# Two graph layers on one core: natural layout of q and k, all score terms as paired half-height products, two head pairs per phase, a new step order

## The chip, the cores and the metric

The kernel runs on one core of one Trainium2 chip. The metric is device time in microseconds of one execution. Engines are named as the profile does: PE is TensorE, DVE is VectorE, ACT is ScalarE, POOL is GpSimd, SP issues the DMAs.

## The reference

64 samples of 256 nodes with 512 features, one 256x256 adjacency for all. Two layers, each with a residual and a layer norm:

```
mi, mj = x @ Wi.T, x @ Wj.T                      # W = [Wi | Wj]
h = layernorm(x + deg * (mi + b) + adj @ mj)
q, k, v = h @ Wq.T + bq, h @ Wk.T + bk, h @ Wv.T + bv   # 8 heads of 64
p = softmax(where(adj == 0, -inf, q @ k.T / 8))
out = layernorm(h + (p @ v) @ Wo.T + bo)
```

All in float32.

## The kernel before

Each float32 operand of a product is kept as two parts in the reduced format (hi and lo), and a product is three: hi*hi, lo*hi, hi*lo (`product`, L349 is the one line that issues them). P = 128 rows, R = 2 row tiles of a sample, C = 4 column tiles, G = 4 groups g of two heads (i = 0, 1), HALF = 64 rows is one head.

One step b works on two samples, and its previous one: the attention of sample b, the first layer and the projections q, k, v of sample n = b + 1, and the output product y and norm of sample b - 1. Every engine runs a list of helpers written out by hand (`step`), and they meet at semaphores only. `steps` runs step 0 without y, then 62 more in a loop or behind it, the last of them without loading ahead, and `last_step` finishes the attention of sample 63. The prologue loads and splits the weights and makes sample 0's h, q, k, v.

PE's order within a step decides when everything is needed: mj, mi (x times Wj, Wi), aggregate (adjacency times mj), transpose_h, q, k, v, y; and for each group of heads scores, transpose_p, attend. PSUM has eight banks: three for the projections in turn, two for scores (one a head), two for transposed probabilities (`pt`), one for `av`.

How a group of heads goes: scores on PE; `maxima` on DVE adds the mask, takes the row maximum, and makes exp_bias; `exponentials` on ACT (four activations of 128x256); `inverse_sums` on DVE; the even head is normalised on ACT, the odd on POOL; transpose_p on PE; `pt_high` on ACT and `pt_low` on DVE make hi and lo; attend on PE; then `o_low_part` (ACT), `o_sum` (DVE, into the single buffer oT), `o_high` (ACT), `split_o` (POOL). `o_sum` of group g waits until `split_o` of group g - 1 has read oT:

```
dve.wait_ge(o_part_done, G * b + g + 1)
if not (first and g == 0):
    dve.wait_ge(o_split, G * b + g)
```

For h: `agg_sum`, `norm_stats`, `norm_mean` on DVE, `root` on POOL, `norm_apply` on DVE, transpose_h on PE, `hT_high` on ACT, `hT_low` on DVE, and q on PE, which waits for both halves:

```
if half == 0:
    pe.wait_ge(read["hT"], 2 * n + 2)
```

POOL also splits the next x transposed: `xT_high` and `split_xT` of sample b + 2.

Layout of q and k before: for each head q_both holds hi on the head's own 64 rows and lo on the other 64; k_twice holds hi on both, the second copy made by DMA (`copy_k`, four a step). So one product of full height gives hi*hi + lo*hi (L475), and a product of half height adds q hi times k lo (L480). The order of the step of PE before stands in the diff.

## Time and profile before

| what | value |
|---|---|
| median of 3 runs | 3146.48 us (3145.89 to 3148.19) |
| span of the profiled execution, first to last instruction | 3145.9 us |
| busy: PE, DVE, ACT, POOL | 3097.3, 2451.1, 1960.7, 1154.5 us |
| weight loads of PE | 2715.3 us |
| mean granted clock of PE | 0.993 of full |

A whole time of the profiled execution is not given beside its span; the span stands 0.6 us under the median of the runs. Matmuls are pipelined, so busy PE says only that a product was always in flight. Instructions of a group that follow each other are merged in a timeline; its second column runs from the first start to the last end.

### The profile page before, as it was taken

Reading aid. Unit: us, or ns where it says so; the run is one execution under the profiler, and the core shown is the slowest. Engines: PE = TensorE matmul, PEld = TensorE weight load, DVE = VectorE, ACT = ScalarE, POOL = GpSimd, SP = SyncE. Lnnn points to the kernel's source line nnn. Section 1 sums busy time; section 2 is a strip of 40 time slices with the busy share of each in tenths; the row PEclk is TensorE's granted clock in tenths of the full one; section 3 lists DMA queues with packets and bytes.
Section 4 is the critical chain, followed back from the end, with each engine's and each line's share of the span. In section 5 each row is a group of like instructions: output and inputs, shape, how many; then the busy total and the mean of one; then the engine's idle time right before and its main releaser. Section 6 shows DMA issues by size and latency. Waiting matters only on the chain.

```text
span 3145.9 us, 59689 instructions
## 1 busy us (share of the span) xinstructions
PE 3097.3 (98%) x19456; PEld 2715.3 (86%) x19456; DVE 2451.1 (78%) x6156; ACT 1960.7 (62%) x4999; POOL 1154.5 (37%) x1097
## 2 busy tenths in 40 slices
PE   6999999999999999999999999999999999999997
PEld 5888888888888888888888888888888888888886
DVE  5778778778778787787787787877877878778776
ACT  3656666666566566666665666666656656666665
POOL 2333333433433333334333333333343333333432
PEclk8999999999999999999999999999999999999999
DMA  4011011111110110111111101111111111011110
GB/s 134 25 51 53 27 53 43 37 53 33 47 53 27 53 53 27 53 36 44 53 32 48 53 27 53 49 31 53 33 47 53 29 51 53 27 53 41 39 48 28
DMA packets 109868, 141.95 MB, mean 45 GB/s; under 512 B 7696, under 2 KB 73744, under 8 KB 109840
## 3 DMA queue, kind: packets, MB, share of 16 engines
q1 hardware_dynamic: 109840, 141.59, 15.2%
q8 instruction: 15, 0.25, 0.0%
q14 instruction: 13, 0.11, 0.0%
HBM read 74.46 MB, written 33.55 MB: 34 GB/s over the span
## 4 chain that ended last, share of the span: by engine, by line
PE 98%; DVE 1%; ACT 0%; issue 0%; DMA 0%; POOL 0%; POOLq 0%; DVEq 0%; SPq 0%
PE proj L349 73%; PE av L349 8%; PE pt L492 7%; PE score L475 4%; PE score L480 3%; PE proj L426 2%; DMA probs<-in_w0T 0%; DVE h L875 0%; DVE k_lo L786 0%; DVE probs L808 0%; DVE pT_lo L823 0%; DVE oT L832 0%; DVE wj_lo L927 0%; DVE wo_lo L927 0%; POOL var_eps_h L284 0%
## 5 line engine op out<-in xcount | busy, mean ns | idle before, releaser
L639 ACT ACTIVATE probs<-probs,exp_bias 128x256 f32<-128x256 f32 x1024 | 509.2, 499 | 247.2 <-DVE exp_bias L814 247.2
L292 POOL TENSOR_TENSOR oT_lo<-oT,oT_hi 128x256 fp32r<-128x256 f32 x256 | 189.8, 742 | 949.3 <-ACT oT_hi L669 949.3
L808 DVE CUSTOM_DVE_ANT_0 probs<-score,mask_add 128x256 f32<-128x256 f32 x1024 | 371.6, 420 | 86.2 <-PE score L480 42.2
L259 POOL TENSOR_TENSOR probs<-probs,row_inv 128x512 f32<-128x512 f32 x256 | 267.0, 1043 | 459.3 <-DVE row_inv L819 459.3
L648 ACT ACTIVATE probs<-probs,row_inv 128x256 f32<-128x256 f32 x512 | 234.2, 509 | 236.9 <-DVE row_inv L819 236.9
L655 ACT CAST pT_hi<-pt 128x512 fp32r<-128x512 f32 x512 | 280.4, 587 | 160.3 <-PE av L349 97.1
L823 DVE TENSOR_TENSOR pT_lo<-pt,pT_hi 128x512 fp32r<-128x512 f32 x512 | 333.5, 681 | 6.1 <-ACT pT_hi L655 0.2
L844 DVE SCALAR_TENSOR_TENSOR h<-proj,deg,xb 128x512 f32<-128x512 f32 x128 | 96.0, 751 | 254.2 <-PE proj L349 254.2
L786 DVE SCALAR_TENSOR_TENSOR q_both<-proj,bq_cols,q_both 64x256 fp32r<-64x256 f32 x512 | 247.6, 484 | 56.3 <-ACT q_both L617 48.7
L349 PE MATMUL proj<-hT_hi,wq_hi 128*128 128x256 f32 x1024 | 289.2, 282 | 1.5 <-DVE hT_lo L764 1.5
L349 PE MATMUL proj<-hT_hi,wq_lo 128*128 128x256 f32 x1024 | 289.0, 282 | 0.0
L349 PE MATMUL proj<-hT_lo,wq_hi 128*128 128x256 f32 x1024 | 288.8, 282 | 0.0
L349 PE MATMUL proj<-hT_hi,wk_lo 128*128 128x256 f32 x1024 | 287.9, 281 | 0.0
L349 PE MATMUL proj<-hT_hi,wk_hi 128*128 128x256 f32 x1024 | 287.5, 281 | 0.0
L349 PE MATMUL proj<-hT_lo,wk_hi 128*128 128x256 f32 x1024 | 287.5, 281 | 0.0
L492 PE MATMUL pt<-ident,probs 128*128 128x128 f32 x2048 | 281.8, 276 | 2.5 <-ACT probs L648 2.5
L349 PE MATMUL av<-pT_hi,v_both 128*128 128x256 f32 x1024 | 271.5, 297 | 4.2 <-DVE pT_lo L823 4.2
L832 DVE SCALAR_TENSOR_TENSOR oT<-av,bv_cols,o_part 64x256 f32<-64x256 f32 x512 | 243.0, 475 | 34.1 <-POOL oT_lo L292 24.9
L786 DVE SCALAR_TENSOR_TENSOR k_lo<-proj,bk_cols,k_twice 64x256 fp32r<-64x256 f32 x512 | 247.5, 483 | 18.3 <-ACT k_twice L629 2.3
L349 PE MATMUL av<-pT_lo,v_both 128*128 128x256 f32 x1024 | 255.5, 283 | 0.0
L492 PEld LDWEIGHTS pt<-ident,probs 128*128 128x128 f32 x2048 | 233.4, 142 | 20.6 <-ACT probs L648 3.0
L617 ACT ACTIVATE q_both<-proj,bq_cols 64x256 fp32r<-64x256 f32 x512 | 241.1, 471 | 15.5 <-PE proj L349 7.5
(98 smaller groups left out, 8826.6 us busy)
## 6 DMA issues: line engine op xcount, KB each, us to landing
xT_raw<-in_xT SPq DMA_DIRECT2D x64, 512.0 KB, 4.5
xb<-in_x SPq DMA_DIRECT2D x64, 512.0 KB, 5.2
k_twice<-k_twice SPq DMA_DIRECT2D x256, 128.0 KB, 2.4
out<-hb SPq DMA_DIRECT2D x64, 512.0 KB, 3.3
probs<-in_w0T SPq DMA_DIRECT2D x1, 1024.0 KB, 6.8
hb<-in_w0T SPq DMA_DIRECT2D x1, 1024.0 KB, 9.0
probs<-in_wqT SPq DMA_DIRECT2D x1, 1024.0 KB, 5.5
hb<-in_wkT SPq DMA_DIRECT2D x1, 1024.0 KB, 5.8
```

The source lines that it names most:

```text
L259: pool.tensor_tensor(probs[:, g % 2, 1, :, :], probs[:, g % 2, 1, :, :], row_inv[:, g % 2, R:2 * R].unsqueeze(2).to_broadcast([P, R, N]), ...
L292: pool.tensor_tensor(oT_lo[:, g, :], oT[:, :], oT_hi[:, g, :].bitcast(F32), ALU.subtract).then_inc(o_split, 1)
L349: return pe.matmul(dst, lhsT, rhs, start=start, stop=stop)
L492: last = pe.transpose(dst[:, kt, r * P:(r + 1) * P], probs[:, g % 2, i, r, kt * P:(kt + 1) * P], ident[:, :])
L617: last = nc.scalar.activation(q_both[home, 2 * t + i, :], src[home, :], ACT.Identity, bias=bq_cols[home, t:t + 1])
L639: last = nc.scalar.activation(e, e, ACT.Exp, bias=exp_bias[:, g % 2, s:s + 1], scale=SCALE, accum_out=row_sum[:, g % 2, s:s + 1])
L648: last = nc.scalar.activation(e, e, ACT.Copy, scale=row_inv[:, g % 2, r:r + 1])
L655: nc.scalar.copy(pT_hi[:, i, :, :], pt[i][:, :].rearrange("p (k q) -> p k q", k=R)).then_inc(pt_hi_done, 1)
L786: last = V.scalar_tensor_tensor(out=dst(t, i), in0=src[home, :], scalar=bias[home, t:t + 1], in1=high[home, 2 * t + i, :].bitcast(F32), op ...
L808: last = V.tensor_tensor_reduce(out=probs[:, g % 2, i, r, :], in0=score[i][:, r * N:(r + 1) * N], in1=mask_add[:, r, :], scale=1.0, scalar ...
L823: V.tensor_tensor(pT_lo[:, i, :, :], pt[i][:, :].rearrange("p (k q) -> p k q", k=R), pT_hi[:, i, :, :].bitcast(F32), ALU.subtract).then_in ...
L832: last = V.scalar_tensor_tensor(out=oT[i * HALF:(i + 1) * HALF, :], in0=av[0:HALF, i * N:(i + 1) * N], scalar=bv_cols[:, 2 * g + i:2 * g + ...
```

## The change

q and k lie in natural layout: q_hi, q_lo, k_hi, k_lo, each 128 rows by column tile, two heads one above the other. The bias-and-split helpers work on 128 rows at once, two instructions a half where there were four, and the DMA copies of k are gone. All three terms of a score are half-height products; the two heads of a group are issued in pairs, rows 0 to 63 and 64 to 127, into two banks. `scores` now covers two groups at once (24 products) and is called twice a step. Scores and transposed probabilities share four banks `attn`, two for each group parity: the scores of groups 2 and 3 wait until `pt_low` of group 1 has read its bank. The order of the step changes on PE, ACT, DVE and POOL; the last step's likewise (left out here, with the bank names in maxima, pt_high and pt_low).

```diff
@@ -94,8 +94,9 @@
-        q_both = sb("q_both", [P, HEADS, N], F32R)
-        k_twice = sb("k_twice", [P, HEADS, N], F32R)
+        q_hi = sb("q_hi", [P, C, N], F32R)
+        q_lo = sb("q_lo", [P, C, N], F32R)
+        k_hi = sb("k_hi", [P, C, N], F32R)
         k_lo = sb("k_lo", [P, C, N], F32R)
...
@@ -126,8 +127,8 @@
-        score = [bank(f"score{i}") for i in range(2)]
-        pt = [bank(f"pt{i}") for i in range(2)]
+        attn = [bank(f"attn{i}") for i in range(4)]
         av = bank("av")
...
@@ -190,22 +190,12 @@
...
-            def copy_k(n, half):
...
-                    sp.dma_start(k_twice[(1 - i) * HALF:(2 - i) * HALF, heads, :].bitcast(F32),
-                                 k_twice[i * HALF:(i + 1) * HALF, heads, :].bitcast(F32)).then_inc(k_copied[half], 16)
...
@@ -315,15 +303,15 @@
                 n = b + 1
                 add_bias(n)
                 normalise_odd(b, 0)
+                normalise_odd(b, 1)
                 root("h", n)
-                normalise_odd(b, 1)
-                normalise_odd(b, 2)
                 if ahead: xT_high(b + 2)
                 if ahead: split_xT(b + 2)
                 split_o(b, 0)
+                split_o(b, 1)
+                normalise_odd(b, 2)
                 normalise_odd(b, 3)
                 if y_: root("out", b - 1)
-                split_o(b, 1)
                 split_o(b, 2)
                 residual(n, 1 - parity, stored=y_)
...
@@ -461,32 +449,28 @@
...
-            def scores(b, g, first=False):
-                pe.wait_ge(read["q"], 2 * b + g // 2 + 1)
-                pe.wait_ge(read["k"], 2 * b + g // 2 + 1)
-                pe.wait_ge(k_copied[g // 2], 32 * (b + 1))
-                if not (first and g == 0):
-                    pe.wait_ge(max_done, 2 * (G * b + g))
-                blocks = [(i, r) for i in range(2) for r in range(R)]
-                for i, r in blocks:
-                    head = 2 * g + i
-                    pe.matmul(score[i][:, r * N:(r + 1) * N], q_both[:, head, r * P:(r + 1) * P],
-                              k_twice[:, head, :], start=(r == 0), stop=False, skip_group_check=True)
-                for i, r in [(i, r) for r in range(R) for i in range(2)]:
-                    head, home = 2 * g + i, slice(i * HALF, (i + 1) * HALF)
-                    last = pe.matmul(score[i][:, r * N:(r + 1) * N], q_both[home, head, r * P:(r + 1) * P],
-                                     k_lo[home, g, :], start=False, stop=True, skip_group_check=True)
-                    if r == R - 1:
-                        last.then_inc(score_done, 1)
-            def transpose_p(b, g, i, first=False):
+            def scores(b, pair, first=False):
+                pe.wait_ge(read["q"], 2 * b + pair + 1)
+                pe.wait_ge(read["k"], 2 * b + pair + 1)
+                if not (first and pair == 0):
+                    pe.wait_ge(pt_read, 2 * (G * b + 2 * pair))
+                for g in (2 * pair, 2 * pair + 1):
+                    terms = [(q_hi, k_hi), (q_lo, k_hi), (q_hi, k_lo)]
+                    for r in range(R):
+                        for j, (q_, k_) in enumerate(terms):
+                            for i in range(2):
+                                home = slice(i * HALF, (i + 1) * HALF)
+                                last = pe.matmul(attn[2 * (g % 2) + i][:, r * N:(r + 1) * N],
+                                                 q_[home, g, r * P:(r + 1) * P], k_[home, g, :],
+                                                 start=(r == 0 and j == 0), stop=(j == len(terms) - 1),
+                                                 skip_group_check=True)
+                                if r == R - 1 and j == len(terms) - 1:
+                                    last.then_inc(score_done, 1)
+            def transpose_p(b, g, i):
                 pe.wait_ge((norm_even_done, norm_odd_done)[i], G * b + g + 1)
-                if not (first and g == 0):
-                    pe.wait_ge(pt_read, 2 * (G * b + g) + i - 1)
-                dst = pt[i][:, :].rearrange("p (k q) -> p k q", k=R)
+                dst = attn[2 * (g % 2) + i][:, :].rearrange("p (k q) -> p k q", k=R)
...
@@ -513,34 +497,32 @@
                 scores(b, 0, not y_)
                 mj(n, 1)
                 mi(n, 0)
-                scores(b, 1)
                 mi(n, 1)
+                transpose_p(b, 0, 0)
+                transpose_p(b, 0, 1)
                 aggregate(n, 0)
                 aggregate(n, 1)
-                transpose_p(b, 0, 0, not y_)
-                transpose_p(b, 0, 1, not y_)
-                scores(b, 2)
+                attend(b, 0, not y_)
+                transpose_p(b, 1, 0)
+                transpose_p(b, 1, 1)
                 if y_: y(b - 1, 0)
+                attend(b, 1)
+                scores(b, 1)
                 if y_: y(b - 1, 1)
                 transpose_h(n, 0)
                 transpose_h(n, 1)
-                scores(b, 3)
-                transpose_p(b, 1, 0)
-                transpose_p(b, 1, 1)
-                attend(b, 0, not y_)
                 q(n, 0)
                 q(n, 1)
                 transpose_p(b, 2, 0)
                 transpose_p(b, 2, 1)
-                attend(b, 1)
                 k(n, 0)
+                attend(b, 2)
+                transpose_p(b, 3, 0)
+                transpose_p(b, 3, 1)
                 k(n, 1)
-                transpose_p(b, 3, 0)
-                attend(b, 2)
-                transpose_p(b, 3, 1)
+                attend(b, 3)
                 v(n, 0)
                 v(n, 1)
-                attend(b, 3)
...
@@ -606,29 +586,20 @@
...
-            def q_high(n, half):
+            def biased_high(kind, n, half, bias, dst):
                 heads_used(n, half)
-                act.wait_ge(done["q"], 2 * n + half + 1)
+                act.wait_ge(done[kind], 2 * n + half + 1)
                 for c in range(2):
                     t = 2 * half + c
-                    src = proj[BANK["q"][half]][:, c * N:(c + 1) * N]
-                    for i in range(2):
-                        home = slice(i * HALF, (i + 1) * HALF)
-                        last = nc.scalar.activation(q_both[home, 2 * t + i, :], src[home, :], ACT.Identity,
-                                                    bias=bq_cols[home, t:t + 1])
-                last.then_inc(hi["q"], 1)
+                    last = nc.scalar.activation(dst[:, t, :], proj[BANK[kind][half]][:, c * N:(c + 1) * N],
+                                                ACT.Identity, bias=bias[:, t:t + 1])
+                last.then_inc(hi[kind], 1)
+            def q_high(n, half):
+                biased_high("q", n, half, bq_cols, q_hi)
             def k_high(n, half):
...
+                biased_high("k", n, half, bk_cols, k_hi)
...
@@ -673,37 +645,37 @@
                 mj_high(n, 0)
                 exponentials(b, 0)
                 mj_high(n, 1)
+                exponentials(b, 1)
                 normalise_even(b, 0)
-                exponentials(b, 1)
+                normalise_even(b, 1)
                 pt_high(b, 0, 0, not y_)
-                normalise_even(b, 1)
                 pt_high(b, 0, 1, not y_)
+                o_low_part(b, 0, not y_)
+                pt_high(b, 1, 0)
+                pt_high(b, 1, 1)
+                o_high(b, 0, not y_)
+                o_low_part(b, 1)
                 exponentials(b, 2)
+                o_high(b, 1)
                 hT_high(n, 0)
                 hT_high(n, 1)
+                exponentials(b, 3)
                 normalise_even(b, 2)
-                pt_high(b, 1, 0)
-                pt_high(b, 1, 1)
-                o_low_part(b, 0, not y_)
-                exponentials(b, 3)
                 q_high(n, 0)
+                normalise_even(b, 3)
                 q_high(n, 1)
-                o_high(b, 0, not y_)
-                o_low_part(b, 1)
                 pt_high(b, 2, 0)
                 pt_high(b, 2, 1)
-                normalise_even(b, 3)
                 k_high(n, 0)
-                k_high(n, 1)
-                o_high(b, 1)
+                o_low_part(b, 2)
                 pt_high(b, 3, 0)
                 pt_high(b, 3, 1)
-                o_low_part(b, 2)
+                o_high(b, 2)
+                k_high(n, 1)
+                o_low_part(b, 3)
+                o_high(b, 3)
                 v_high(n, 0)
                 v_high(n, 1)
-                o_high(b, 2)
-                o_low_part(b, 3)
-                o_high(b, 3)
...
@@ -780,33 +752,29 @@
                 dve.wait_ge(hi[kind], 2 * n + half + 1)
                 for c in range(2):
                     t = 2 * half + c
-                    src = proj[BANK[kind][half]][:, c * N:(c + 1) * N]
-                    for i in range(2):
-                        home = slice(i * HALF, (i + 1) * HALF)
-                        last = V.scalar_tensor_tensor(
-                            out=dst(t, i), in0=src[home, :], scalar=bias[home, t:t + 1],
-                            in1=high[home, 2 * t + i, :].bitcast(F32), op0=ALU.add, op1=ALU.subtract)
+                    last = V.scalar_tensor_tensor(
+                        out=dst[:, t, :], in0=proj[BANK[kind][half]][:, c * N:(c + 1) * N], scalar=bias[:, t:t + 1],
+                        in1=high[:, t, :].bitcast(F32), op0=ALU.add, op1=ALU.subtract)
                 last.then_inc(read[kind], 1)
             def q_low(n, half):
-                biased_low("q", n, half, bq_cols, q_both,
-                           lambda t, i: q_both[(1 - i) * HALF:(2 - i) * HALF, 2 * t + i, :])
+                biased_low("q", n, half, bq_cols, q_hi, q_lo)
             def k_low_half(n, half):
-                biased_low("k", n, half, bk_cols, k_twice,
-                           lambda t, i: k_lo[i * HALF:(i + 1) * HALF, t, :])
+                biased_low("k", n, half, bk_cols, k_hi, k_lo)
...
@@ -877,50 +846,50 @@
             def step(b, parity, y_=True, ahead=True):
                 n, other = b + 1, 1 - parity
+                mj_low(n, 0)
                 maxima(b, 0, not y_)
-                mj_low(n, 0)
-                mi_sum(n, 0)
+                maxima(b, 1, not y_)
                 mj_low(n, 1)
                 inverse_sums(b, 0)
-                maxima(b, 1, not y_)
+                mi_sum(n, 0)
+                inverse_sums(b, 1)
                 mi_sum(n, 1)
+                pt_low(b, 0, 0)
+                pt_low(b, 0, 1)
                 agg_sum(n, 0)
                 agg_sum(n, 1)
                 norm_stats("h", n, 0, read["agg"], h_row)
                 norm_stats("h", n, 1, read["agg"], h_row)
-                inverse_sums(b, 1)
                 norm_mean("h", n)
-                maxima(b, 2)
+                o_sum(b, 0, not y_)
+                pt_low(b, 1, 0)
+                pt_low(b, 1, 1)
                 norm_apply("h", n, h_row)
                 if y_: y_sum(b - 1, 0, other)
-                pt_low(b, 0, 0)
-                pt_low(b, 0, 1)
+                o_sum(b, 1)
+                maxima(b, 2)
+                if y_: norm_stats("out", b - 1, 0, read["y"], hb_row[other])
+                maxima(b, 3)
                 if y_: y_sum(b - 1, 1, other)
-                inverse_sums(b, 2)
                 hT_low(n, 0)
                 hT_low(n, 1)
-                maxima(b, 3)
-                if y_: norm_stats("out", b - 1, 0, read["y"], hb_row[other])
-                pt_low(b, 1, 0)
-                pt_low(b, 1, 1)
-                o_sum(b, 0, not y_)
+                inverse_sums(b, 2)
+                if y_: norm_stats("out", b - 1, 1, read["y"], hb_row[other])
+                if y_: norm_mean("out", b - 1)
                 inverse_sums(b, 3)
-                if y_: norm_stats("out", b - 1, 1, read["y"], hb_row[other])
                 q_low(n, 0)
+                if y_: norm_apply("out", b - 1, hb_row[other])
                 q_low(n, 1)
-                o_sum(b, 1)
                 pt_low(b, 2, 0)
                 pt_low(b, 2, 1)
-                if y_: norm_mean("out", b - 1)
                 k_low_half(n, 0)
+                o_sum(b, 2)
+                pt_low(b, 3, 0)
+                pt_low(b, 3, 1)
                 k_low_half(n, 1)
-                pt_low(b, 3, 0)
-                o_sum(b, 2)
-                pt_low(b, 3, 1)
-                if y_: norm_apply("out", b - 1, hb_row[other])
+                o_sum(b, 3)
                 v_low(n, 0)
                 v_low(n, 1)
-                o_sum(b, 3)
```

## Rows read from the trace of the kernel before

**Rows 1.** The page, part 4: share of the chain that ended last.

```profile
PE 98%; DVE 1%; ACT 0%; issue 0%; DMA 0%; POOL 0%; POOLq 0%; DVEq 0%; SPq 0%
```

**Rows 2.** The chain in order of time: start us, us, what.

```profile
1480.28 5.79 PE proj L349 x24
1528.44 5.79 PE proj L349 x24
```

**Rows 3.** Timeline of PE, a score group: start us, us, what, idle before.

```profile
1514.02 0.64 PE L475 MATMUL score<-k_twice,q_both 128*128 128x256 f32 x4
1514.59 0.50 PE L480 MATMUL score<-k_lo,q_both 64*128 64x256 f32 x4
1515.02 0.50 PE L349 MATMUL proj<-wj_hi,xT_hi 128*128 128x512 f32 x1
1515.36 0.39 PE L349 MATMUL proj<-wj_hi,xT_lo 128*128 128x512 f32 x1
```

**Rows 4.** Line 480 in 1510 to 1524: ns min/median/max.

```profile
L480 PE MATMUL score<-k_lo,q_both x8: 277/330/383, 1514.6 to 1521.5; 64*128 64x256 f32 x8
```

**Rows 5.** Timeline of ACT.

```profile
1534.70 1.07 ACT L589 CAST hT_hi<-proj 128x512 fp32r<-128x512 f32 x2 [1.57 <-PE proj L426]
...
1540.55 0.51 ACT L639 ACTIVATE probs<-probs,exp_bias 128x256 f32<-128x256 f32 x1 [0.80 <-DVE exp_bias L814]
...
1542.45 0.19 ACT L639 ACTIVATION_READ_ACCUMULATOR probs<-probs,exp_bias 128x1 f32 x1
1542.66 3.87 ACT L617 ACTIVATE q_both<-proj,bq_cols 64x256 fp32r<-64x256 f32 x8
```

**Rows 6.** Timeline of DVE.

```profile
1522.43 0.40 DVE L808 CUSTOM_DVE_ANT_0 probs<-score,mask_add 128x256 f32<-128x256 f32 x1
...
1523.90 0.17 DVE L814 TENSOR_SCALAR exp_bias<-row_max 128x4 f32<-128x4 f32 x1
...
1526.69 0.69 DVE L850 TENSOR_TENSOR h<-proj,h 128x512 f32<-128x512 f32 x1 [0.25 <-PE proj L349]
1527.30 1.27 DVE L864 BATCH_NORM_STATS2 stats_h<-h 128x6 f32<-128x512 f32 x2
...
1528.68 0.25 DVE L870 BATCH_NORM_AGGREGATE mean_var_h<-stats_h 128x2 f32<-128x6 f32 x2
...
1532.45 1.27 DVE L823 TENSOR_TENSOR pT_lo<-pt,pT_hi 128x512 fp32r<-128x512 f32 x2
...
1535.32 1.29 DVE L764 TENSOR_TENSOR hT_lo<-proj,hT_hi 128x512 fp32r<-128x512 f32 x2 [0.28 <-ACT hT_hi L589]
...
1542.22 0.96 DVE L832 SCALAR_TENSOR_TENSOR oT<-av,bv_cols,o_part 64x256 f32<-64x256 f32 x2
...
1544.62 3.99 DVE L786 SCALAR_TENSOR_TENSOR q_both<-proj,bq_cols,q_both 64x256 fp32r<-64x256 f32 x8 [0.65 <-ACT q_both L617]
```

**Rows 7.** Timeline of PE, transpose_h.

```profile
1534.07 1.04 PE L426 MATMUL proj<-ident,h 128*128 128x128 f32 x8
```

**Rows 8.** Timeline of POOL.

```profile
1529.28 0.70 POOL L287 TENSOR_TENSOR rstd_h<-var_eps_h,power_cols 128x2 f32<-128x2 f32 x1
...
1536.12 1.90 POOL L252 TENSOR_TENSOR xT_hi<-xT_raw,zero 128x1024 fp32r<-128x1024 f32 x1
1538.10 2.39 POOL L265 TENSOR_TENSOR xT_lo<-xT_raw,xT_hi 128x1024 fp32r<-128x1024 f32 x1
1547.04 0.73 POOL L292 TENSOR_TENSOR oT_lo<-oT,oT_hi 128x256 fp32r<-128x256 f32 x1 [6.55 <-ACT oT_hi L669]
```

**Rows 9.** Timeline of DVE in the prologue.

```profile
34.30 4.58 DVE L875 TENSOR_SCALAR h<-h,mean_var_h,rstd_h 128x512 f32<-128x512 f32 x2 [0.87 <-POOL rstd_h L287]
```

**Rows 10.** Timeline of PE in the first step.

```profile
86.50 1.97 PE L426 MATMUL proj<-ident,h 128*128 128x128 f32 x8 [3.55 <-DVE h L875]
```

**Rows 11.** PE by stretches: window, length, busy us (instructions), granted clock, DMA share, GB/s.

```profile
84.00:86.00 2.00, 0.00 (x0) 0.92 0.00 0
...
92.00:94.00 2.00, 2.00 (x17) 0.87 0.00 0
```

More of the change, by code:

```diff
@@ L191, in store @@
                 sp.dma_start(out_rows[b, :, :, :], hb[:, parity, :, :]).then_inc(out_stored, 16)
-            def copy_k(n, half):
-                sp.wait_ge(hi["k"], 2 * n + half + 1)
-                for i in range(2):
-                    heads = slice(4 * half + i, 4 * half + i + 3, 2)
-                    sp.dma_start(k_twice[(1 - i) * HALF:(2 - i) * HALF, heads, :].bitcast(F32),
-                                 k_twice[i * HALF:(i + 1) * HALF, heads, :].bitcast(F32)).then_inc(k_copied[half], 16)
             def step(b, parity, y_=True, ahead=True):
@@ L333, in last_step @@
                 normalise_odd(b, 1)
+                split_o(b, 0)
+                split_o(b, 1)
                 normalise_odd(b, 2)
-                split_o(b, 0)
                 normalise_odd(b, 3)
+                split_o(b, 2)
                 root("out", b - 1)
-                split_o(b, 1)
-                split_o(b, 2)
                 split_o(b, 3)
@@ L562, in last_step @@
                 scores(b, 0)
-                scores(b, 1)
+                y(b - 1, 0, tail=True)
                 transpose_p(b, 0, 0)
                 transpose_p(b, 0, 1)
-                scores(b, 2)
-                y(b - 1, 0, tail=True)
-                scores(b, 3)
+                attend(b, 0)
                 transpose_p(b, 1, 0)
                 transpose_p(b, 1, 1)
-                attend(b, 0)
                 y(b - 1, 1, tail=True)
+                scores(b, 1)
+                attend(b, 1)
                 transpose_p(b, 2, 0)
-                attend(b, 1)
                 transpose_p(b, 2, 1)
@@ L655, in pt_high @@
                 nc.scalar.copy(pT_hi[:, i, :, :],
-                               pt[i][:, :].rearrange("p (k q) -> p k q", k=R)).then_inc(pt_hi_done, 1)
+                               attn[2 * (g % 2) + i][:, :].rearrange("p (k q) -> p k q",
+                                                                     k=R)).then_inc(pt_hi_done, 1)
             def o_low_part(b, g, first=False):
@@ L734, in last_step @@
                 normalise_even(b, 1)
-                exponentials(b, 2)
-                normalise_even(b, 2)
+                o_low_part(b, 0)
                 pt_high(b, 1, 0)
                 pt_high(b, 1, 1)
-                o_low_part(b, 0)
+                o_high(b, 0)
+                exponentials(b, 2)
+                o_low_part(b, 1)
+                normalise_even(b, 2)
                 exponentials(b, 3)
-                o_high(b, 0)
-                o_low_part(b, 1)
+                o_high(b, 1)
                 pt_high(b, 2, 0)
                 pt_high(b, 2, 1)
-                o_high(b, 1)
                 normalise_even(b, 3)
@@ L808, in maxima @@
                         last = V.tensor_tensor_reduce(
-                            out=probs[:, g % 2, i, r, :], in0=score[i][:, r * N:(r + 1) * N],
+                            out=probs[:, g % 2, i, r, :], in0=attn[2 * (g % 2) + i][:, r * N:(r + 1) * N],
                             in1=mask_add[:, r, :], scale=1.0, scalar=MASKED, op0=ALU.add, op1=ALU.max,
@@ L822, in pt_low @@
                 dve.wait_ge(pt_hi_done, 2 * (G * b + g) + i + 1)
-                V.tensor_tensor(pT_lo[:, i, :, :], pt[i][:, :].rearrange("p (k q) -> p k q", k=R),
+                V.tensor_tensor(pT_lo[:, i, :, :],
+                                attn[2 * (g % 2) + i][:, :].rearrange("p (k q) -> p k q", k=R),
                                 pT_hi[:, i, :, :].bitcast(F32), ALU.subtract).then_inc(pt_read, 1)
@@ L970, in last_step @@
                 maxima(b, 1)
+                y_sum(b - 1, 0, 0)
                 inverse_sums(b, 1)
-                maxima(b, 2)
                 pt_low(b, 0, 0)
                 pt_low(b, 0, 1)
-                y_sum(b - 1, 0, 0)
+                norm_stats("out", b - 1, 0, read["y"], hb_row[0])
+                o_sum(b, 0)
+                pt_low(b, 1, 0)
+                pt_low(b, 1, 1)
+                maxima(b, 2)
                 inverse_sums(b, 2)
                 maxima(b, 3)
-                pt_low(b, 1, 0)
-                pt_low(b, 1, 1)
-                o_sum(b, 0)
-                norm_stats("out", b - 1, 0, read["y"], hb_row[0])
-                y_sum(b - 1, 1, 0)
+                o_sum(b, 1)
                 inverse_sums(b, 3)
-                norm_stats("out", b - 1, 1, read["y"], hb_row[0])
-                norm_mean("out", b - 1)
-                o_sum(b, 1)
                 pt_low(b, 2, 0)
                 pt_low(b, 2, 1)
-                norm_apply("out", b - 1, hb_row[0])
+                y_sum(b - 1, 1, 0)
+                norm_stats("out", b - 1, 1, read["y"], hb_row[0])
                 o_sum(b, 2)
+                norm_mean("out", b - 1)
                 pt_low(b, 3, 0)
                 pt_low(b, 3, 1)
+                norm_apply("out", b - 1, hb_row[0])
                 o_sum(b, 3)
```

16 lines of the change are left out of this document (removed).

## The prediction

> **What bounds the kernel now.** I read the chain that ended last first: TensorE (PE) holds 98% of it [rows 1]. Two equal pieces of the loop, a step apart, stand 48.16 us from each other [rows 2]. So a step costs what its TensorE instructions cost, end to end, and everything else is cover. The 24 products in that piece take 5.79 us with the last one lasting 0.40, so a product of 512 columns comes every 0.234 us [rows 2]. Two questions decide: does TensorE get less to do, and does the new order still keep every other engine ahead of it?
>
> **TensorE's work.** One group of scores before: four full-height products start at 14.02, four half-height ones at 14.59, the next block at 15.02, whose first product takes 0.34 us to the next start instead of 0.234 [rows 3]. That is 1.00 + 0.11 = 1.11 us a group, 4.44 a step. The full ones come every (0.64 - 0.28)/3 = 0.12 us. The half-height ones are the question. Their record is 0.50 us for four, the longest 383 ns, the shortest 277 [rows 3, 4]: four in a row at 0.12 would need 0.28 + 3 x 0.12 = 0.64, so two run side by side, and the second pair ends 0.50 - 0.383 = 0.117 us behind the first. The extra 0.106 of the long ones is a weight load laid bare when the height changes. What is left of the 1.11, after 4 x 0.12 and 2 x 0.117, is 0.40: two changes of height at 0.20 each.
> After: 24 half-height products a phase are 12 pairs, 12 x 0.117 + 0.40 = 1.80 us, twice a step 3.60. TensorE gets 0.84 us less a step: 47.32 us. All of it comes from two phases instead of four, that is 4 changes of height fewer (0.80); the products themselves come out even (6 slots a group before and after). Bounds: a pair at 0.12 gives -0.77; a pair at 0.222, if weight loads could not hide behind the pair before, gives +1.7.
> The rule that speaks against this: the Trainium skill, "TensorE: Matmul & The Clock Gate", part 3 (packing small matmuls), says a weight load overlaps running matmuls only where the row group differs. By that rule every second pair would lay its load bare, 0.117 + 0.106 = 0.22 us a pair, and the sum would be 5.3 + 0.8 = 6.1 us a step instead of 3.60. The row of this kernel has the second pair 0.117 us behind the first in the same row groups, so I go by the row; it is one sample of two pairs, and so a rival.
>
> **ScalarE, VectorE, queues.** q_high and k_high fall from 16 activations a step to 8, the lows likewise: eight of q take 3.87 us on ScalarE and eight 3.99 on VectorE [rows 5, 6], and the same for k, so each engine loses about 3.9 us a step. They lie beside TensorE and are worth nothing there by themselves. In the prologue they stand on the chain: half of one q_high, of one q_low and of k_low is about 4 us, once. Four k copies a step leave the SP queue; what was queued behind them (store, next xT and x loads) only goes earlier, and I give it nothing.
>
> **The new order.** Here I laid the steps out one behind the other. Mark zero is the end of the first transpose_p of group 0. TensorE's own work from there to the end of transpose_h is: second transpose 4 x 0.11 = 0.44 (eight take 1.04, the last 0.28: 0.11 each [rows 7]), aggregate 8 x 0.234 = 1.87, attend 0 0.95, transposes of group 1 0.87, y0 2.81, attend 1 0.95, scores 1.80, y1 2.81, transpose_h 0.87. Sum 13.37 us. And q(n,0) now stands directly behind transpose_h, where before scores(3), two transposes and attend(0) lay between (1.11 + 0.87 + 0.95, 2.9 us of products). q waits for hT_lo.
> The work that leads to hT_lo, from the same mark:
> - pt_high 0.03 + 0.59 (a cast of 128x512; two take 1.07 [rows 5]): 0.62.
> - VectorE without a pause: pt_low twice, 1.2 (two in 1.27), to 1.85; agg_sum twice, 0.61 to the next start each, to 3.06; norm_stats twice, done at 4.33; norm_mean 0.11 + 0.25, done at 4.69 [rows 6].
> - root("h") on POOL: norm_mean's end (1528.93) to rstd's end (1529.98) is 1.05: 5.74 [rows 6, 8].
> - Now POOL has xT_high and split_xT next, 1536.12 to 1540.49, 4.37 us: 10.11. Only then split_o(0), 0.73: 10.84 [rows 8]. Before, these two sat in a quiet place behind normalise_odd(2), and split_o(0) had a wide margin to its reader.
> - o_sum(1) waits for split_o(0), because oT is one buffer, and in VectorE's order maxima(2) stands behind o_sum(1). o_sum 0.06 + 0.9: 11.80 [rows 6]. Meanwhile VectorE sits in norm_apply("h"): in the prologue, under the very same xT_high and split_xT, its two instructions took 4.58 us [rows 9] instead of about 1; this blocking ends when split_xT does, so it costs nothing beyond the gate of split_o(0).
> - maxima(2): 1522.43 to 1523.90 + 0.17 = 1.64 [rows 6]: bias at 13.44. Then on VectorE norm_stats 0.6, maxima(3) 1.6, y_sum(1) 0.6: free at 16.2. On ScalarE exponentials(2) 1540.55 to 1542.64, 2.09: 15.56; o_high(1) 0.3, an estimate from the activations of the same width less their fixed part: 15.85; hT_high(0) 0.59, hT_high(1) 0.48 more: 16.95.
> - hT_low(0) from 16.4, hT_low(1) from 17.0, done at 17.7 [rows 6]; q's first product is late by hand-over 0.07, bare weight load 0.106 and its own length 0.277, less the 0.12 it would take anyway: 0.33. Together 18.03 us.
> TensorE stands 18.03 - 13.37 = 4.66 us a step. A few tenths of it fall before attend(1), whose pt_low(1,1) stands behind the same VectorE run; nearly all before q. The other waits just hold. Transposes of group 0: counted from the end of mj(0), mj_high and mj_low take 1.25, maxima(0) 1.64, exponentials(0) 2.1, mj_high(1) 0.5, exponentials(1) 2.0, normalise_even about 1.0 (half an exponentials), together 8.5; TensorE arrives after 1.80 + 3 x 2.81 = 10.2. The same count leaves attend 0, 2 and 3 a few tenths each, so the rest of the step adds nothing in my layout; plus or minus 0.5 for hand-overs.
> The Trainium skill, "SBUF — State Buffer", section on the two separate sides, has VectorE's two-port instructions and GpSimd lock each other out for a whole instruction; [rows 9] agrees, and by rule and row the sum is the same here.
>
> **The clock.** In the first step of before TensorE stood 3.55 us ahead of transpose_h, until 86.50 [rows 10]. The granted clock averages 0.92 in 84 to 86 and 0.87 in 92 to 94 [rows 11], so it was at half (1.2 of 2.4 GHz) from about 85.7 to 92.5; about 6.0 us of products ran in it and lost 3.0. A stall of over 4 us in every step will do the same again and again, and the products behind it (q, k, then the next step up to the transposes) are on the loop. Bounds per step 0 and 3.0; I take 1.7, since with a longer stall more of the low stretch lies inside the idleness, and only dense products follow.
>
> **Sum.** 47.32 + 4.66 + 1.7 = 53.7 us a step against 48.16: +5.5. 62 full steps: +343 us; prologue -4; the last two steps I leave as they are (plus or minus 10). The profiled span of 3145.9 stands 0.6 us under the median of 3146.48, so 3146.5 + 343 - 4 = 3486 us. A change under 0.2% (6 us) could not be told from none.
>
> **Rivals.**
> 1. The gate through split_o, with the clock falling: 3486 us, its own range 3420 to 3550. Chance 0.52.
> 2. The same gate, but the clock holds or nearly: +3.8 x 62, about 3380. For it: stalls shorter than a microsecond or so leave the clock alone; against it: 3.55 us did not. 0.17.
> 3. Only the direct conversion shows: hT_high and hT_low behind transpose_h take 0.59 + 0.48 + 0.69 + 0.33 less the half transpose already over (0.44), 1.7 us, if POOL gets to split_o earlier than laid out or maxima slip ahead. Then 47.3 + 1.7 + 0.3 = 49.3, 3220 without and 3320 with the clock. 0.13.
> 4. Weight loads of pairs lie bare (0.22 us a pair): the first phase lies on the loop, +1.3 a step; the second is absorbed by the stall. 3565. 0.12.
> 5. The other side: all waits are covered and the 0.84 us remain, 3146 - 52 - 4 = 3090. This needs hT_lo done 0.3 us before transpose_h ends; the conversion alone forbids it by 1.7 us, so it decides only if TensorE is late elsewhere. 0.03. Near no change, the two cancelling (stall under 0.9 us): 0.03.
> Faster 0.03, same 0.02, slower 0.95. The range runs from the upper part of rival 3 to rival 4: 3320 to 3575.
>
> **What would show it.** Per step: an idle stretch of TensorE of 4 to 5 us before the first q product, released by hT_lo of VectorE; VectorE's norm_apply("h") in pairs far over 1 us; oT on VectorE waiting for oT_lo of POOL; TensorE's clock under 1 in the middle slices; two score groups a step with pairs ending 0.12 us apart. Wrong if split_o(0) is done before VectorE comes to o_sum(1), if the stall lies before attend or the transposes instead, if pairs end 0.22 us apart, or if the granted clock stays at 1.0.

## The result and the profile after

The changed kernel takes 3767.7 us against 3146.7 us: a ratio of 1.1975 (95% interval 1.1961 to 1.1989), 19.7% slower. The forecast was slower, 3486 us, with 3575 as its upper end; the time lies 282 us above it.

The chain that ended last, first line of the page's part 4, the one that gave TensorE 98% before [rows 1]:

```profile
PE 73%; DVE 14%; ACT 6%; issue 4%; POOL 2%; DMA 0%; DVEq 0%; SPq 0%; POOLq 0%; ACTq 0%
```

So 27% of that chain is no longer TensorE's. Two pieces of the chain in order of time (start us, us, what), 41 steps apart:

```profile
236.15 8.59 PE proj L337 x36
...
2614.87 8.59 PE proj L337 x36
```

(2614.87 - 236.15) / 41 = 58.02 us a step, against 48.16 [rows 2]: 9.86 more, and 62 such steps are 611 of the 621 us. The loop explains the change; prologue and last steps are small. Timeline of PE in one step (idle before, and its releaser, in brackets):

```profile
1527.97 0.39 PE L337 MATMUL proj<-wo_lo,oT_hi 128*128 128x512 f32 x1
1528.47 0.38 PE L337 MATMUL av<-pT_hi,v_both 128*128 128x256 f32 x1
1528.69 0.28 PE L337 MATMUL av<-pT_lo,v_both 128*128 128x256 f32 x1
...
1529.61 0.39 PE L464 MATMUL attn<-k_hi,q_hi 64*128 64x256 f32 x2
1529.84 0.28 PE L464 MATMUL attn<-k_hi,q_lo 64*128 64x256 f32 x2
...
1531.02 0.28 PE L464 MATMUL attn<-k_lo,q_hi 64*128 64x256 f32 x2
1531.23 0.50 PE L337 MATMUL proj<-wo_hi,oT_hi 128*128 128x512 f32 x1
...
1533.90 0.39 PE L337 MATMUL proj<-wo_lo,oT_hi 128*128 128x512 f32 x1
1534.13 1.03 PE L414 MATMUL proj<-ident,h 128*128 128x128 f32 x8
1542.70 0.58 PE L337 MATMUL proj<-hT_hi,wq_hi 128*128 128x256 f32 x1 [7.53 <-DVE hT_lo L736]
1543.08 0.42 PE L337 MATMUL proj<-hT_hi,wq_lo 128*128 128x256 f32 x1
...
1547.99 0.34 PE L337 MATMUL proj<-hT_hi,wq_hi 128*128 128x256 f32 x1
```

Three things stand here. The scores of two groups run from 1529.61 to 1531.23, the first product behind them takes 0.11 us longer to the next start than the usual 0.234, and a change of height begins ahead of 1529.61 (0.09 us by the same count as in [rows 3]). The pair starts lie 0.12 us apart from the second pair on: the products cost what was forecast, 1.8 us a phase. Then transpose_h ends its stream, and TensorE stands 7.53 us until hT_lo is there. And q's first product takes 0.58 us, where 0.38 is what it takes behind a wait at the full clock (in e4 below): it runs at half the clock.

What happens during those 7.53 us is read on ScalarE, which had been idle before o_high(0) too:

```profile
1521.46 1.07 ACT L626 CAST pT_hi<-attn 128x512 fp32r<-128x512 f32 x2 [1.30 <-PE attn L476]
...
1534.33 0.41 ACT L641 CAST oT_hi<-oT 128x256 fp32r<-128x256 f32 x1 [7.92 <-PE proj L337]
1534.76 0.58 ACT L634 COPY o_part<-av 64x512 f32<-64x512 f32 x1
1538.35 0.51 ACT L610 ACTIVATE probs<-probs,exp_bias 128x256 f32<-128x256 f32 x1 [3.00 <-DVE exp_bias L782]
...
1540.33 0.39 ACT L641 CAST oT_hi<-oT 128x256 fp32r<-128x256 f32 x1
1540.74 1.07 ACT L569 CAST hT_hi<-proj 128x512 fp32r<-128x512 f32 x2
```

The bracket of the second row is the finding: o_high(0) (oT_hi) was released by PE proj, that is by y(b-1,1), whose last product ends at 1534.29 (1533.90 + 0.39), not by oT on VectorE. On POOL (same step) xT_lo was long over when split_o(0) came:

```profile
1529.20 2.45 POOL L253 TENSOR_TENSOR xT_lo<-xT_raw,xT_hi 128x1024 fp32r<-128x1024 f32 x1
1534.82 0.72 POOL L280 TENSOR_TENSOR oT_lo<-oT,oT_hi 128x256 fp32r<-128x256 f32 x1 [3.16 <-ACT oT_hi L641]
```

And on VectorE, from o_sum(0) on:

```profile
1526.12 0.97 DVE L801 SCALAR_TENSOR_TENSOR oT<-av,bv_cols,o_part 64x256 f32<-64x256 f32 x2
...
1528.33 3.61 DVE L844 TENSOR_SCALAR h<-h,mean_var_h,rstd_h 128x512 f32<-128x512 f32 x2
1531.86 0.68 DVE L825 TENSOR_TENSOR hb<-proj,hb 128x512 f32<-128x512 f32 x1
1535.64 0.97 DVE L801 SCALAR_TENSOR_TENSOR oT<-av,bv_cols,o_part 64x256 f32<-64x256 f32 x2 [3.11 <-POOL oT_lo L280]
1536.64 0.42 DVE L776 CUSTOM_DVE_ANT_0 probs<-attn,mask_add 128x256 f32<-128x256 f32 x1
...
1538.14 0.17 DVE L782 TENSOR_SCALAR exp_bias<-row_max 128x4 f32<-128x4 f32 x1
...
1540.47 0.69 DVE L825 TENSOR_TENSOR hb<-proj,hb 128x512 f32<-128x512 f32 x1
1541.36 1.29 DVE L736 TENSOR_TENSOR hT_lo<-proj,hT_hi 128x512 fp32r<-128x512 f32 x2 [0.20 <-ACT hT_hi L569]
```

o_sum(0) had oT ready at 1527.09, 7.2 us before o_high(0) took it. norm_apply took 3.61 us beside POOL's xT pair, as in [rows 9], y_sum(0) followed, and then o_sum(1) waited 3.11 us for split_o(0). Everything behind it in VectorE's order came late: maxima(2), maxima(3), y_sum(1), hT_low. PE by stretches of 2 us (window, length, busy, granted clock, DMA share, GB/s):

```profile
1536.00:1538.00 2.00, 0.00 (x0) 0.97 0.00 0
...
1542.00:1544.00 2.00, 1.30 (x6) 0.50 0.00 0
...
1548.00:1550.00 2.00, 2.00 (x18) 0.97 0.00 0
```

The clock is at half from just before 1538 to just past 1548 (0.97 in 1548 to 1550 is 0.12 us at half); half of q's products run in it.

The step adds up. From the end of transpose_h (1534.13 + 1.03) to the end of q's first product (1542.70 + 0.58) are 8.12 us, 8.0 more than the 0.12 it would take anyway. Of these, 0.2 are the clock (0.58 us instead of 0.38) and 7.8 are standing. attend(1) adds 0.37 of standing: its first product starts 0.50 us behind the last one of y(b-1,0) instead of 0.234, and takes 0.22 to the next start instead of 0.12. Together 8.2 us of standing. The 23 starts from 1543.08 to 1547.99 lie 0.213 us apart instead of 0.118, 2.2 us in all; with the 0.2 of the first product the clock costs 2.4. The products take 47.4, by e7 below: 47.4 + 8.2 + 2.4 = 58.0.

### The profile page after: what moved, and what is told of

Its sections match the earlier page's. It is cut to its first block, busy times and chain, and to the rows that moved or that the text cites. A ratio compares the mean times of both kernels' runs of the same rounds, so it can differ in the third digit from the quotient of the medians.

```text
span 3765.8 us, 59564 instructions
## 1 busy us (share of the span) xinstructions
PE 3232.9 (86%) x20480; PEld 2836.7 (75%) x20480; DVE 2209.1 (59%) x5644; ACT 1682.8 (45%) x4487; POOL 1159.8 (31%) x1097
## 4 chain that ended last, share of the span: by engine, by line
PE 73%; DVE 14%; ACT 6%; issue 4%; POOL 2%; DMA 0%; DVEq 0%; SPq 0%; POOLq 0%; ACTq 0%
PE proj L337 58%; PE attn L464 5%; PE av L337 5%; PE attn L476 4%; ACT probs L610 3%; DVE pT_lo L791 3%; DVE probs L776 2%; DVE hT_lo L736 2%; DVE h L819 2%; DVE stats_h L833 2%; DVE oT L801 2%; POOL oT_lo L280 1%; ACT oT_hi L641 1%; ACT hT_hi L569 1%; ACT pT_hi L626 1%
## 5 line engine op out<-in xcount | busy, mean ns | idle before, releaser
L337 PEld LDWEIGHTS proj<-hT_hi,wq_hi 128*128 128x128 f32 x1024 | 270.6, 264 | 492.3 <-DVE hT_lo L736 490.4
L776 DVE CUSTOM_DVE_ANT_0 probs<-attn,mask_add 128x256 f32<-128x256 f32 x1024 | 371.5, 419 | 14.1 <-PE attn L464 3.4
L641 ACT CAST oT_hi<-oT 128x256 fp32r<-128x256 f32 x256 | 102.8, 402 | 577.1 <-PE proj L337 495.4
L755 DVE SCALAR_TENSOR_TENSOR q_lo<-proj,bq_cols,q_hi 128x256 fp32r<-128x256 f32 x256 | 112.1, 479 | 399.1 <-ACT q_hi L594 399.1
L791 DVE TENSOR_TENSOR pT_lo<-attn,pT_hi 128x512 fp32r<-128x512 f32 x512 | 329.5, 685 | 26.3 <-ACT pT_hi L626 22.3
L626 ACT CAST pT_hi<-attn 128x512 fp32r<-128x512 f32 x512 | 275.1, 591 | 88.9 <-PE attn L476 85.6
L476 PE MATMUL attn<-ident,probs 128*128 128x128 f32 x2048 | 268.0, 274 | 8.7 <-ACT probs L619 5.2
L337 PEld LDWEIGHTS proj<-hT_hi,wq_lo 128*128 128x128 f32 x1024 | 268.9, 263 | 0.0
L337 PEld LDWEIGHTS proj<-hT_lo,wq_hi 128*128 128x128 f32 x1024 | 264.8, 259 | 0.0
L594 ACT ACTIVATE q_hi<-proj,bq_cols 128x256 fp32r<-128x256 f32 x256 | 107.3, 470 | 318.0 <-PE proj L337 318.0
```

The costliest lines, as they stand in the source:

```text
L337: return pe.matmul(dst, lhsT, rhs, start=start, stop=stop)
L476: last = pe.transpose(dst[:, kt, r * P:(r + 1) * P], probs[:, g % 2, i, r, kt * P:(kt + 1) * P], ident[:, :])
L626: nc.scalar.copy(pT_hi[:, i, :, :], attn[2 * (g % 2) + i][:, :].rearrange("p (k q) -> p k q", k=R)).then_inc(pt_hi_done, 1)
L641: nc.scalar.copy(oT_hi[:, g, :], oT[:, :]).then_inc(o_hi_done, 1)
L755: last = V.scalar_tensor_tensor(out=dst[:, t, :], in0=proj[BANK[kind][half]][:, c * N:(c + 1) * N], scalar=bias[:, t:t + 1], in1=high[:, t ...
L776: last = V.tensor_tensor_reduce(out=probs[:, g % 2, i, r, :], in0=attn[2 * (g % 2) + i][:, r * N:(r + 1) * N], in1=mask_add[:, r, :], scal ...
```

## The experiments

Two theories. A: the gate in front of o_sum(1) is o_high(b,0), which waits for the end of y(b-1,1), since y(b-1) still reads oT_hi and oT_lo:

```python
if g == 0 and not first:
    act.wait_ge(done["y"], R * b)
```

B, the prediction's own: POOL's xT_high and split_xT, put ahead of split_o(0), are the gate by themselves.

**e1_two_oT.** Two slots in turn for groups 0 and 1; a wait for y remains ahead of group 2, which has one slot:

```diff
-        oT_hi = sb("oT_hi", [P, G, N], F32R)
+        oT_hi = sb("oT_hi", [P, G + 2, N], F32R)
...
+        def slot(g, par):
+            return g if g >= 2 or par == 0 else G + g
...
-                if g == 0 and not first:
+                if g == 2 and not (type(b) is int and b == 0):
                     act.wait_ge(done["y"], R * b)
```

> The changed kernel with two slots in turn for groups 0 and 1 of oT_hi and oT_lo, so that o_high(b,0) no longer waits until y(b-1,1) has read them. Theory A (the gate in front of o_sum(1) is o_high(0), which waits for the end of y(b-1,1)): o_sum(1) comes free when split_xT ends, about 3.1 us a step earlier; TensorE's idle time before q falls from 7.5 to 4.4 us; 3767 - 61 x 3.1 = about 3578 us, plus or minus 60 for the clock. Theory B (the prediction's: POOL's xT_high and split_xT ahead of split_o(0) are the gate by themselves): nothing changes, 3767 us.

Measured 3556.6 us, ratio 1.1301 (1.1282 to 1.1320). POOL and PE in one of its steps:

```profile
1502.89 2.46 POOL L256 TENSOR_TENSOR xT_lo<-xT_raw,xT_hi 128x1024 fp32r<-128x1024 f32 x1
1505.31 0.92 POOL L283 TENSOR_TENSOR oT_lo<-oT,oT_hi 128x256 fp32r<-128x256 f32 x1
```

```profile
1513.39 0.58 PE L340 MATMUL proj<-hT_hi,wq_hi 128*128 128x256 f32 x1 [4.46 <-DVE hT_lo L739]
```

Now split_o(0) follows split_xT without a gap: the prediction's gate exists, but in the changed kernel it opened first (xT_lo ends at 1531.65) and o_high(0) held the way for another 3.2 us. Without the later gate the idle time before q is 4.46 us. A holds, B by itself does not.

**e2_pool_order.** split_o ahead of the xT pair, nothing else:

```diff
                 root("h", n)
+                split_o(b, 0)
+                split_o(b, 1)
                 if ahead: xT_high(b + 2)
                 if ahead: split_xT(b + 2)
-                split_o(b, 0)
-                split_o(b, 1)
                 normalise_odd(b, 2)
```

> The changed kernel with split_o(0) and split_o(1) moved ahead of xT_high and split_xT on POOL, nothing else. Theory A: the end of y(b-1,1) still releases o_high(0), so the time stays within 0.5% of 3767 us although norm_apply of h is no longer held up (its pair falls from 3.6 to about 1 us). Theory B: the gate opens 4.3 us earlier, about 3500 us.

Measured 3765.6 us, 1.1964 (1.1944 to 1.1984): unchanged. norm_apply of h fell from 3.61 to 0.99 us, and o_sum(1) waited 5.72 us for split_o(0) instead of 3.11. What norm_apply had lost beside POOL's xT pair fell into a time of waiting anyway. B, as the one cause, falls.

**e3_both.** Both edits.

> Both edits together: two slots for oT of groups 0 and 1, and split_o ahead of the xT pair. Theory A: the two gates lie one behind the other, so only now both are open; VectorE and ScalarE still run maxima(2), maxima(3), exponentials(2), hT_high and hT_low behind the scores; idle before q about 2.4 us, 3400 us plus or minus 60 for the clock. Theory B: the same as the pool order alone.

Measured 3342.0 us, 1.0620 (1.0603 to 1.0638), at the lower end of what was forecast. From 200 to 3000 us the granted clock, read in stretches of 1 us, falls 33 times, each time for 3.4 us. Steps with such a fall take 51.8 us, the others 50.3. TensorE's waits there, over 54 steps (who waited for whom, us in total, times, longest):

```profile
PE proj L340 <- DVE hT_lo L739: 120.3, 54, 2.2
```

2.2 us a step are left: the conversion of h itself and the maxima, exponentials and y_sum that stand in line ahead of it. e2's edit is worth nothing alone and 215 us behind e1's.

**e4_fill.** To price the clock alone: 20 products a step that nobody reads, between transpose_h and q.

```diff
+            def fill(b):
+                pe.wait_ge(av_read, G * b + 2)
+                for i in range(20):
+                    mm(av[:, :], w_hi["wk"][:, 0, 0:P], w_hi["wk"][:, 1, :], True, True)
...
                 transpose_h(n, 1)
+                fill(b)
                 q(n, 0)
```

> The changed kernel with 20 further products of 512 columns a step on TensorE between transpose_h and q, of weights into the bank av, whose result nobody reads; they start when o_sum(1) has read av (4.7 us of products in the idle stretch of 7.5 us). Clock theory (the halved clock over the first 5.5 us of q costs 2.7 us a step): the clock stays at full, q starts at the same time and runs faster, 3767 - 61 x 2.7 = about 3602 us, though there are 1280 products more. Rival (the low clock lies in the shade of some other wait): no gain, 3767 us or more.

Measured 3617.1 us, 1.1493 (1.1474 to 1.1512): 1260 products more make the kernel 150 us faster than the changed one. PE in one step:

```profile
1530.55 1.03 PE L414 MATMUL proj<-ident,h 128*128 128x128 f32 x8
1533.13 4.85 PE L337 MATMUL av<-wk_hi 128*128 128x512 f32 x20 [1.55 <-DVE oT L807]
1539.17 0.38 PE L337 MATMUL proj<-hT_hi,wq_hi 128*128 128x256 f32 x1 [1.19 <-DVE hT_lo L742]
```

transpose_h to q is 8.62 us, as good as the 8.57 of the changed kernel (1534.13 to 1542.70): the fill moved nothing. But q's first product takes 0.38 us, not 0.58. PE from 200 to 3400 us, this kernel and then the changed one (clock behind the busy time):

```profile
200.00:3400.00 3200.00, 3039.45 (x19583) 1.00 0.09 29
```

```profile
200.00:3400.00 3200.00, 2771.99 (x17612) 0.91 0.08 27
```

So of the step's 9.86 us, 2.4 (150 us over 62 steps) are the clock; the rest is 8.2 of standing still less 0.7 of cheaper products.

**e5_y_early.** Only TensorE's order: y(b-1,1) directly behind y(b-1,0).

```diff
                 if y_: y(b - 1, 0)
+                if y_: y(b - 1, 1)
                 attend(b, 1)
                 scores(b, 1)
-                if y_: y(b - 1, 1)
```

> The changed kernel with y(b-1,1) issued right behind y(b-1,0) on TensorE, ahead of attend(1) and scores(1), nothing else: no buffer and no other engine's order is touched. Theory A (o_high(0) is held by the end of y(b-1,1)): that end comes 2.8 us earlier, o_sum(1) as well, but the scores of groups 2 and 3 come 2.8 us later; q starts about 2 to 2.8 us earlier, 3767 - 61 x 2.5 = about 3615 us, less again if the low stretch of the clock shortens (down to 3560). Theory B (POOL's xT pair is the gate): 3767 us, since POOL's order is the same.

Measured 3556.6 us, 1.1299 (1.1281 to 1.1316), a little under the lower end that was forecast (3560). Moving the product that nobody seemed to wait for takes 211 us off, with POOL as it was. A holds again.

**e6_layout_only.** The kernel before, its order and banks, with the natural layout and the three paired terms, one group a phase.

```diff
-                blocks = [(i, r) for i in range(2) for r in range(R)]
...
+                terms = [(q_hi, k_hi), (q_lo, k_hi), (q_hi, k_lo)]
+                for r in range(R):
+                    for j, (q_, k_) in enumerate(terms):
+                        for i in range(2):
```

> The kernel before with the new layout alone: q_hi, q_lo, k_hi, k_lo in natural layout, three half-height products a term in pairs, no copies of k, but one group a phase, two score banks and the whole step order of before. Theory A (pairs end 0.117 us apart, a change of height costs 0.20 twice a phase): a group costs 6 x 0.117 + 0.40 = 1.10 us as before, so only the prologue gains, 3142 us, plus or minus 5. Rival (pairs lay their weight loads bare, 0.22 each): +2.5 us a step, 3300 us.

Measured 3143.2 us, ratio 0.9989 (0.9980 to 0.9998), within 0.2%. One group of scores on PE:

```profile
1507.85 0.39 PE L463 MATMUL score<-k_hi,q_hi 64*128 64x256 f32 x2
1508.07 0.28 PE L463 MATMUL score<-k_hi,q_lo 64*128 64x256 f32 x2
...
1508.54 0.28 PE L463 MATMUL score<-k_lo,q_hi 64*128 64x256 f32 x2
1508.76 0.50 PE L337 MATMUL proj<-wj_hi,xT_hi 128*128 128x512 f32 x1
1509.09 0.39 PE L337 MATMUL proj<-wj_hi,xT_lo 128*128 128x512 f32 x1
```

1507.85 to 1508.76 is 0.91, and the next product takes 0.34 to the following start instead of 0.234: 1.02 us a group. By starts this is under the 1.10 expected, since part of the first change of height lies ahead of 1507.85; a whole step takes 48.15 us, as before. The layout costs and gives nothing in the loop, as worked out. The first score products of step 0 start at 63.73 us, against 68.55 before, so the 4 us that the whole gains come from the prologue. The rival with bare weight loads is out.

**e7_reordered.** Can the change be kept without its waits? e3 with y(b-1,1) between transpose_h and q (q's banks swapped, so that only its second half waits until y is read), the conversion of h ahead of what does not hurry, and POOL's xT pair later. The edit is shown against e3's kernel; lines of moved helpers are left out where they stood.

```diff
-                "q": (1, 2), "k": (0, 1), "v": (2, 1)}
+                "q": (2, 1), "k": (0, 1), "v": (2, 1)}
...
                 if y_: root("out", b - 1)
+                if y_: pool.wait_ge(normed["out"], R * b)
+                if ahead: xT_high(b + 2)
+                if ahead: split_xT(b + 2)
...
                     pe.wait_ge(read["hT"], 2 * n + 2)
+                else:
                     if type(n) is not int or n >= 2:
...
-                    pe.wait_ge(read["q"], 2 * n + 1)
+                    pe.wait_ge(read["q"], 2 * n + 2)
...
                 scores(b, 1)
-                if y_: y(b - 1, 1, 1 - parity)
                 transpose_h(n, 0)
                 transpose_h(n, 1)
+                if y_: y(b - 1, 1, 1 - parity)
...
+                hT_high(n, 0)
+                hT_high(n, 1)
                 exponentials(b, 2)
...
                 maxima(b, 2)
+                hT_low(n, 0)
+                hT_low(n, 1)
```

> The changed kernel with two slots for oT of groups 0 and 1, y(b-1,1) between transpose_h and q on TensorE (q's banks swapped so that only its second half waits for y), hT_high ahead of exponentials(2), hT_low ahead of maxima(3), and the xT pair on POOL behind root of out and norm_apply of out. Theory A (all that the change lost is the waiting in front of q and the clock that falls with it; the products themselves are 0.84 us a step cheaper): TensorE never waits in a steady step, the clock stays at full, 47.3 us a step, 3146 - 62 x 0.84 - 4 = about 3090 us. Rival (shared banks or two groups a phase cost something of their own): above 3146 us.

Measured 3127.8 us, ratio 0.9932 (0.9918 to 0.9945): faster than before by 0.7%, 640 us under the changed kernel, but 38 us over the 3090 expected. A step takes 47.75 us (mean of six), and TensorE does wait once in it (weight loads):

```profile
1517.96 0.19 PEld L341 LDWEIGHTS av<-pT_hi,v_both 128*128 128x128 f32 x1 [0.51 <-DVE pT_lo L796]
```

That is attend(1), about 0.33 us end to end; without it the products are 47.4 us, 0.74 under before. The loop gains 0.41 x 62 = 25 us; 20 are left in the whole, so some 5 are given back outside it, where 4 from the prologue had been expected on top. A part lies at the end: from 3050 us on TensorE is granted 0.80 of its clock on average, against 0.92 in the kernel before. One of the five runs took 3121.5 us, at a mean granted clock of 0.994 instead of 0.991. I did not take these stretches apart further.

**e8_attend_early.** e7 with o_sum(0) and pt_low(1) ahead of norm_stats(1) and norm_mean on VectorE, and y_sum(0) ahead of norm_apply; the edit is shown against e7's kernel.

```diff
-                norm_stats("h", n, 1, read["agg"], h_row)
-                norm_mean("h", n)
                 o_sum(b, 0, not y_)
                 pt_low(b, 1, 0)
                 pt_low(b, 1, 1)
-                norm_apply("h", n, h_row)
+                norm_stats("h", n, 1, read["agg"], h_row)
+                norm_mean("h", n)
                 if y_: y_sum(b - 1, 0, other)
+                norm_apply("h", n, h_row)
```

> The reordered kernel with o_sum(0) and pt_low(1) moved ahead of the second norm_stats of h and norm_mean on VectorE, and y_sum(0) ahead of norm_apply. Theory A (the one wait left in a steady step is attend(1) for pt_low(1,1), 0.33 us end to end, the same that the prediction laid out): it goes, 47.4 us a step, 3128 - 62 x 0.33 = about 3107 us. Rival (norm_apply now comes too late for transpose_h): the wait moves there and the time stays at 3128 us or rises.

Measured 3142.2 us, 0.9987 (0.9978 to 0.9996): the rival. The one wait has become two:

```profile
1526.55 0.86 PEld L418 LDWEIGHTS proj<-ident,h 128*128 128x128 f32 x8 [0.40 <-DVE h L849]
...
1530.33 0.19 PEld L341 LDWEIGHTS proj<-hT_hi,wq_hi 128*128 128x128 f32 x1 [0.32 <-DVE hT_lo L741]
```

norm_apply, now 0.4 us late, holds transpose_h, and hT_low behind it holds q.

**e9_one_oT.** e7 with one slot again: `slot` returns g, and o_high(b,0) waits for y(b-1,1).

> The reordered kernel with the second slots of oT taken out of use again, so that o_high(b,0) waits for the end of y(b-1,1) as in the changed kernel; all else as reordered. Theory A (that one wait, and what stands behind it on ScalarE, is the gate, wherever y stands): y now ends 2.8 us behind transpose_h, and o_high(0), o_low(1), the two hT_high and hT_low follow it, so TensorE idles some 2.7 us before q; with the clock about +3 to +5.5 us a step, 3310 to 3470 us. Rival (the second slot was not needed once the order is right): 3128 us.

One run, 3549.0 us, 421 over e7. A's mechanism, but the time lies 80 us above my range. PE's wait before q, then ScalarE and VectorE ahead of it:

```profile
1508.13 0.58 PE L341 MATMUL proj<-hT_hi,wq_hi 128*128 128x256 f32 x1 [5.31 <-DVE hT_lo L741]
```

```profile
1502.91 0.40 ACT L646 CAST oT_hi<-oT 128x256 fp32r<-128x256 f32 x1 [8.78 <-PE proj L341]
1503.34 0.58 ACT L639 COPY o_part<-av 64x512 f32<-64x512 f32 x1
1503.94 1.07 ACT L574 CAST hT_hi<-proj 128x512 fp32r<-128x512 f32 x2
```

```profile
1504.22 0.97 DVE L806 SCALAR_TENSOR_TENSOR oT<-av,bv_cols,o_part 64x256 f32<-64x256 f32 x2 [6.61 <-POOL oT_lo L283]
...
1506.72 0.17 DVE L787 TENSOR_SCALAR exp_bias<-row_max 128x4 f32<-128x4 f32 x1
1506.80 1.28 DVE L741 TENSOR_TENSOR hT_lo<-proj,hT_hi 128x512 fp32r<-128x512 f32 x2
```

I had counted o_high(0), o_low(1), hT_high and hT_low, 2.7 us. But on VectorE o_sum(1) and maxima(2) stand ahead of hT_low and wait for split_o(0) as well: 5.31 us. The same oversight as in the prediction, one engine further on.

## Why the prediction was wrong, point by point

- **TensorE's products: right.** 47.32 us a step forecast; e7 without its wait has 47.4, and with that the changed kernel's step adds up. Pairs end 0.12 us apart in rows of twelve, so the row weighed against the Trainium skill's rule on row groups ("TensorE: Matmul & The Clock Gate", part 3) stands.
- **Where TensorE waits: right.** Before q, for hT_lo, with a few tenths before attend(1).
- **The step that failed** is in the list of works that lead to hT_lo: "Only then split_o(0), 0.73: 10.84". It took for granted that split_o(0)'s own input was there. Up to that gate the layout held: counted from the same mark (1521.43, the end of the first transpose_p, 0.03 us ahead of pt_high at 1521.46), POOL's xT pair ends at 10.2 against 10.11. But split_o(0) starts at 13.4. o_high(b,0) waits for the end of y(b-1,1), which lay 9 us ahead of its need in the old order (y ends before transpose_h at 1534.07 [rows 7], oT is ready at 1542.22 + 0.96 [rows 6]), because attend(0) came behind both y products. In the new order attend(0) and o_high(0) come ahead of y(b-1,1), and the margin is gone and more: o_high(0) starts at 1534.33, some 7 us after oT was ready. I followed what each moved helper hands on, and did not look up the wait that o_high has on the reader of its buffer. 4.66 us of standing a step were forecast, 8.2 measured, and the missed wait is 3.2 of the difference. With that one wait removed (e1) the idle stretch is 4.46 us, a step takes 54.6 us and the whole 3557 us, 70 over the forecast: 0.9 us a step, about 0.4 of them standing and 0.4 the clock.
- **The clock: right in kind, small in size.** 1.7 us taken of a range from 0 to 3.0; 2.4 by the profile and by e4.
- **The sum of the miss:** 58.0 - 53.7 = 4.3 us a step, 3.5 from the standing (mostly the missed wait), 0.7 from the clock and 0.1 from the products; 62 times 4.3 are 267 of the 282 us. The prologue's 4 us were right: step 0's first scores start at 64.12 us, against 68.55 before.
- **Rivals:** none had the mechanism, and the range ended at a rival that was only about weight loads. The sign "oT on VectorE waiting for oT_lo of POOL" came true and proved nothing, since split_o(0) was late for another reason than the one forecast; only what released o_high(0) tells the two apart. The rival with bare weight loads fell (e6). That VectorE's blocked norm_apply costs nothing beyond the gate was right (e2).

## What to carry to other kernels

When an order is changed, list for each moved helper not only what it waits for as data, but who must have read the buffer that it overwrites: here 211 of the 621 us lost went with one guard against overwriting (e1), on which nothing had waited in the old order, and 421 us in the better order (e9 against e7). Two gates in line show only the later one, so an edit that opens the earlier one measures as nothing (e2) and is worth 215 us once the later is open (e3). And a stall of some microseconds on TensorE can be paid twice, the second time in the clock of the products behind it.

## What the runs showed of the hardware beyond that

- Standing and the clock do not simply add. e1, e5 and e9 idle 4.46, 5.07 and 5.31 us before q, and their steps all take 54.6 us. The granted clock, read in stretches of 1 us, is at half for 6.8, 6.8 and 3.4 us of each step, and TensorE works in 4.6, 4.2 and 3.0 of these: the more it stands, the less it loses by the clock. Why the three sums agree this closely was not found out.
- Twenty useless products in an idle stretch made the products behind them faster by 2.4 us a step.
- Idle stretches of 2.2 us can still cost clock: in e3 33 of them from 200 to 3000 us were followed by 3.4 us at half, at a price of 1.5 us each (51.8 us a step against 50.3), and the others were not. In e4 stretches of 1.55 and 1.19 us cost none: the granted clock is 1.00 from 200 to 3400 us.
- A change between full and half height on TensorE costs about 0.2 us, also when twelve pairs follow: 1.8 us a phase less 12 x 0.12 leaves 0.4 for two changes. Two groups a phase save four changes a step, and e7's products take 0.73 us less than the 48.15 of e6.
